# Moving three VectorE operations within a step of a gated attention block

## The chip, the cores and the metric

The kernel runs on one core of a Trainium2 chip. The metric is the device time of one execution in microseconds (us), the median of several runs.

## The reference

The input x is 2048 tokens x 512. It is normalised (layer norm) and goes through two branches, whose product is added to x.

```python
q, k, v = (_causal_dwconv(_silu(x @ W), conv_w) for each)   # 16 heads of 128, 4 taps
z, a, b = x @ Wz, x @ Wa, x @ Wb
q = q * cos + rot_half(q) * sin;  k = k * cos + rot_half(k) * sin
q = q / max(norm(q), 1e-12);      k = k / max(norm(k), 1e-12)
for s in range(4):                                          # lags 0 to 3
    attn = einsum('bshd,bshd->bsh', q, lag(k, s)) * scale
    gate = sigmoid(lag(a, s) * b)
    out = out + (attn * gate)[..., None] * lag(v, s)
out = out * rsqrt(mean(out * out) + eps) * norm_w * silu(z)
attn_branch = out @ Wout
ffn_branch  = (relu((x @ sign(up).T) * up_scale) @ sign(down).T) * down_scale * output_scale
x = x + attn_branch * silu(ffn_branch)
```

Each token looks at four keys only: its own and the three before it.

## The kernel before

The attention part, which takes the first two thirds of the time, works in steps. A step is one head h (16 of them) and one chunk g of 512 tokens (4 of them): 64 steps, numbered c = 4 h + g. The steps of the first two heads and of the last one are written out; those between are in a loop over the heads on every engine. Each engine has its own list of operations per step (the functions `step`), and semaphores tie the lists together. A chunk passes through several steps: in step c the projections are those of chunk c, while what comes behind them belongs to chunks c-1 to c-4.

- TensorE (`on_tensor`, L997, L1042, L1054, L1066), in step c: project q, k and v of chunk c (12 matmuls of 512 columns each, a product of split numbers in three parts), `turn_fold` (L1054: it turns the squares of chunk c-1), project z of chunk c-2, `sum_values` (L1042: values times coefficients of chunk c-3, both in float32), `score` (L1066: keys times queries of chunk c-2, blocks of 128 keys x 132 queries). `sum_values` waits for `coef_done`, the mask of the same chunk. `score` waits for `gated` of the chunk before, since both use one bank.
- ScalarE: SiLU of each projection out of PSUM (L662), a halo of three columns, the first tap as a scaled copy (L676), squares of q and k (L703, L704), SiLU of z (L711), a copy of the spill (L688).
- VectorE (`on_vector`): the remaining three taps of q, k and v (`conv_tap`, L812; called q1 to q3, k1 to k3, v1 to v3 here), the turn of v (L852), the products with cosine and sine (`rope`, L831 and L835), `sum_fold` (L842: reads the turned squares from PSUM and sums them to 4 norms for q and 4 for k per token row), `gate_scores` (L858: scores in PSUM times gates, into `coef`), `mask_band` (L867: `coef` times a band of ones), `join_out`, `make_o` and, in a head's last step, three splits of weights (L823), in its second step one.
- GpSimd (`on_gpsimd`): `roots` (L528 sets a floor under the norms, L532 raises to the power -1/2; it waits for `norms_done` of L842), `gate_keys` (L537), and in the next step the issues of accumulating DMAs (`fold_squares` L568, `add_swapped` L574 for rot_q and rot_k, `add_squares` L562), and between those of q and k `make_gates` (L548, L551, L556), which gives `gates_done`.
- SyncE's queue: `store_rq` (L402, L403, L405: the roots of chunk c-1 go to `rq_scratch` in DRAM), `load_rq` (L412: they come back shifted by rows for chunk c-2), which waits until the three stores have landed. Then the stores of o and the loads of v.

`make_gates` in step c handles chunk c-3 and needs the load of step c-1, which needs the roots of step c-1. `gate_scores` in step c needs those gates.

The order on each engine is written out by hand. Behind the attention come the FFN with the signs of the weights, and the output projection. They don't take part in the change.

Of the kernel before, what the change touches and what calls it, by code (L numbers as in the profile page):

```python
# [205 lines left out]
def attention(nc, env):  # L206
# [135 lines left out]
    def back(h, g, k):  # L342

        h2, g2 = (h, g - k) if g >= k else (h - 1, g - k + G)
        if isinstance(h2, int) and not 0 <= h2 < H:
            return None
        return h2, g2
# [11 lines left out]
    def is_start(h, g):  # L359
        return isinstance(h, int) and h == 0 and g == 0  # L360

    def is_end(h, g):
        return is_last(h) and g == G - 1

    def is_last(h):
        return isinstance(h, int) and h >= H - 1
# [404 lines left out]
    def on_vector(dve):  # L771
# [34 lines left out]
        def conv_tap(n, i, h, g, c):  # L806

            if i == 1:
                wait(dve, tap_done[n], c + 1)
            else:  # L810
                wait(dve, conv_done[n], DVE_TAPS[n] * c + i - 1)
            nc.vector.scalar_tensor_tensor(  # L812
                y[n][:, g % 2, :], u[n][:, g % 2, i:i + CH], cw[n][:, bass.ds(h * TAPS + i, 1)],
                y[n][:, g % 2, :], ALU.mult, ALU.add).then_inc(conv_done[n], 1)

        def join_out(g3, c):
            wait(dve, spill_saved, c - 2)
            nc.vector.tensor_tensor(out_begin, out_begin, carry[:, 2 * g3:2 * g3 + 2, :], ALU.add
                                    ).then_inc(out_joined, 1)

        def split_lo(n, h):
            wait(dve, whi_done[n], h + 1)
            nc.vector.tensor_tensor(w_lo[n][:, :, :], raw[n][:, :, :], w_hi[n][:, :, :].bitcast(fp32),  # L823
                                    ALU.subtract).then_inc(wlo_done[n], 1)

        def rope(n, i, g, c):

            wait(dve, conv_done[n], 3 * c + 3)
            if i == 0:
                wait(dve, scores_done, c - 3)  # L830
                op = nc.vector.tensor_tensor(rot[n][:, cols(g)], y[n][:, g % 2, :], cos[:, cols(g)], ALU.mult)  # L831
            else:
                if not (isinstance(c, int) and c < 2):
                    wait_rope(dve, n, g, c - 2)
                op = nc.vector.tensor_tensor(swapped[n][:, g % 2, :], y[n][:, g % 2, :], sin[:, cols(g)],  # L835
                                             ALU.mult)
            op.then_inc(rope_done[n], 1)

        def sum_fold(g1, c):
            wait(dve, turned_f, c)  # L840
            wait(dve, root_done, c - 2)
            nc.vector.tensor_reduce(norms[:, g1 % 2, :].rearrange("p (n b) -> p b n", b=BC),  # L842
                                    bank_tk[:, :].rearrange("p (b n d) -> p b n d", b=BC, n=2),
                                    AxisListType.X, ALU.add).then_inc(norms_done, 1)

        def turn_v(g1, k):

            wait(dve, conv_done["v"], 3 * (k + 1))
            if not (isinstance(k, int) and k < 2):
                wait_v(dve, g1, k - 2)  # L850
            v = y["v"][:, g1 % 2, :]
            nc.vector.transpose(v, v).then_inc(v_turned, 1)  # L852

        def gate_scores(g2, k):
            wait(dve, scores_done, k + 1)
            wait(dve, out_done, k - 1)
            wait(dve, gates_done, k + 1)
            nc.vector.tensor_tensor(  # L858
                coef[:, g2 % 2, :, :].rearrange("p b (a r) -> p b a r", r=LAGS),
                scores.rearrange("p b (a r) -> p b a r", r=LAGS),  # L860
                gates[:, :, None, :].broadcast_to([P, BC, BW // LAGS, LAGS]),
                ALU.mult).then_inc(gated, 1)

        def mask_band(g2, k):
            w = coef[:, g2 % 2, :, :]
            wait(dve, gated, k + 1)
            nc.vector.tensor_tensor(w, w, band[:, None, :].broadcast_to([P, BC, BW]), ALU.mult  # L867
                                    ).then_inc(coef_done, 1)

        def make_o(h3, g3, k):  # L870
            wait(dve, out_joined, k + 1)
            wait(dve, z_done, k + 1)

            wait(dve, o_stored[g3 % 2], 16 * (k // 2) if isinstance(k, int) else 8 * k - (8 if g3 % 2 else 0))
            nc.vector.scalar_tensor_tensor(
                o_buf[:, g3 % 2, :].rearrange("p (a n) -> p a n", a=2), out_sums,
                nw_sb[:, bass.ds(h3, 1)], z_act[:, g3 % 2, :].rearrange("p (a n) -> p a n", a=2),
                ALU.mult, ALU.mult).then_inc(o_done, 1)

        def step(h, g):  # L880
            c = h * G + g
            at1, at3 = back(h, g, 1), back(h, g, 3)
            conv_tap("q", 1, h, g, c)
            if at1:
                turn_v(at1[1], c - 1)
                rope("k", 0, at1[1], c - 1)
            conv_tap("q", 2, h, g, c)
            if at1:
                rope("k", 1, at1[1], c - 1)
            conv_tap("q", 3, h, g, c)  # L890
            conv_tap("k", 1, h, g, c)
            if at1:
                sum_fold(at1[1], c)
            conv_tap("k", 2, h, g, c)
            if at3:
                gate_scores(at3[1], c - 3)
                mask_band(at3[1], c - 3)
            conv_tap("k", 3, h, g, c)
            if is_start(h, g):
                dve.wait_ge(ab_turned, 1)  # L900
                nc.vector.tensor_copy(ab, bank_ab.rearrange("p (b n) -> p b n", b=NB)).then_inc(ab_done, 1)
                nc.vector.memset(bx[:, NB, :, :], 0.0).then_inc(bx_done, 1)
                dve.wait_ge(ab_done, 1)
                dve.wait_ge(const_in, 16)
                for r in range(LAGS):
                    nc.vector.tensor_scalar(bx[:, 0:NB, :, r], ab[:, :, H:AB], period[:, r:r + 1], None, ALU.mult
                                            ).then_inc(bx_done, 1)
            if is_start(h, g - 1):
                for i in range(2):
                    blocks = slice(i * HALF_NB, (i + 1) * HALF_NB)  # L910
                    dve.wait_ge(picked, i + 1)
                    nc.vector.tensor_tensor(
                        gate0[:, blocks, :].rearrange("p b (h r) -> p b h r", h=H),
                        pick_banks[i].rearrange("p (b h r) -> p b h r", b=HALF_NB, h=H),
                        ab[:, blocks, 0:H][:, :, :, None].broadcast_to([P, HALF_NB, H, LAGS]),
                        ALU.mult).then_inc(prod_done, 1)
            if g == 3 and not is_last(h):
                split_lo("q", h + 1)
            conv_tap("v", 1, h, g, c)
            if is_start(h, g):  # L920
                dve.wait_ge(tables_in, 32)
            rope("q", 0, g, c)
            conv_tap("v", 2, h, g, c)
            if at3:
                join_out(at3[1], c)
            conv_tap("v", 3, h, g, c)
            if g == 3 and not is_last(h):
                split_lo("k", h + 1)
            if at3:
                make_o(at3[0], at3[1], c - 3)  # L930
            rope("q", 1, g, c)
            if is_end(h, g):
                dve.wait_ge(squares_done, NC)
                nc.vector.tensor_tensor(fold[g % 2], fold[g % 2], other[g % 2], ALU.add).then_inc(folded_last, 1)
            if g == 3 and not is_last(h):
                split_lo("v", h + 1)
            if is_start(h, g - 1):
                for i in range(2):
                    part = gate0[:, i * HALF_NB:(i + 1) * HALF_NB, :]
                    dve.wait_ge(tanh_done, i + 1)  # L940

                    nc.vector.tensor_scalar(part, part, 1.0, 0.5 * SCALE, ALU.add, ALU.mult
                                            ).then_inc(gate_done, 1)
            if g == 1 and not (isinstance(h, int) and h == 0):
                split_lo("z", h)

        schedule(dve, step)
        turn_v(G - 1, NC - 1)
        rope("k", 0, G - 1, NC - 1)
# [656 lines left out]
```

## Time and profile before

| | |
|---|---|
| median of 3 runs | 1353.47 us (1352.22 to 1355.14) |
| the profiled execution | 1353.56 us |
| its span | 1351.7 us |
| TensorE busy | 1304.4 us, 96% |
| VectorE busy | 953.5 us, 71% |
| ScalarE busy | 720.7 us, 53% |
| GpSimd busy | 638.7 us, 47% |
| granted TensorE clock, mean | 0.996 of full speed |
| steps of the attention | 64, up to about 920 us |

The engines are named PE (TensorE), DVE (VectorE), ACT (ScalarE), POOL (GpSimd) and SP (SyncE); SPq is SyncE's queue. A line such as L858 is that of the kernel's file, where the operation is issued. The granted clock stands at its upper level in 39 or so of the page's 40 slices. In the attention part VectorE's busy share is about nine tenths, later two to four tenths.

### The profile page before, as it was taken

What the parts mean: (1) busy time and instruction counts of PE and PEld (TensorE: products, weight loads), DVE (VectorE), ACT (ScalarE), POOL (GpSimd) and SP (SyncE); (2) the same over time, 40 slices, a digit from 0 to 9 for tenths busy, and PEclk for the clock granted to TensorE, in tenths of its full rate; (3) what the DMA queues carried; (4) which work ended last, traced back from release to release, by engine and by line L of the source; (5) the groups of instructions that cost most, each with busy time, mean ns of one, the idle gap of its engine ahead of it and who ended that gap; (6) DMA issues with size and microseconds to landing.
All of it is one profiled execution on the core that took longest, in us unless ns stands there. A gap on an engine that the chain in (4) does not pass through costs nothing.

```text
span 1351.7 us, 22085 instructions
## 1 busy us (share of the span) xinstructions
PE 1304.4 (96%) x6312; PEld 1076.0 (80%) x6312; DVE 953.5 (71%) x1530; ACT 720.7 (53%) x1377; POOL 638.7 (47%) x827
## 2 busy tenths in 40 slices
PE   6989999999999999999999999998999999999998
PEld 5678888787878878888878888887888888888886
DVE  7888998989898998989898998985122223334342
ACT  5655665656666656566565666665543444422221
POOL 6367666767676666767666667765000000000001
PEclk9999999999999999999999999998999999999999
DMA  8368878878787877787787878677710101156544
GB/s 262 65 124 155 168 134 166 161 144 162 136 172 147 154 145 153 159 162 144 154 161 147 163 131 172 129 138 174 245 40 24 47 16 55 52 182 202 176 128 141
DMA packets 276876, 188.89 MB, mean 140 GB/s; under 512 B 167905, under 2 KB 204769, under 8 KB 276577
## 3 DMA queue, kind: packets, MB, share of 16 engines
q1 hardware_dynamic: 238064, 121.48, 32.8%
q0 software_dynamic: 38768, 66.87, 30.9%
q8 instruction: 23, 0.38, 0.1%
q14 instruction: 21, 0.16, 0.1%
HBM read 79.36 MB, written 42.08 MB: 90 GB/s over the span
## 4 chain that ended last, share of the span: by engine, by line
PE 51%; DVE 27%; issue 11%; ACT 6%; POOL 2%; DMA 2%; DVEq 1%; SPq 0%; POOLq 0%; ACTq 0%
PE bank L1491 13%; PE bank L997 11%; PE bank L1294 8%; PE bank L1281 8%; DVE y_q L812 6%; DVE y_k L812 6%; PE bank L1042 4%; PE bank L1066 3%; ACT y_q L676 3%; DVE rot_k L831 3%; DVE coef L858 3%; DVE coef L867 3%; ACT u_q L662 2%; DVE y_v L812 1%; DVEq L80 1%
## 5 line engine op out<-in xcount | busy, mean ns | idle before, releaser
L812 DVE SCALAR_TENSOR_TENSOR y_q<-u_q,cw_q,y_q 128x512 f32<-128x512 f32 x192 | 143.3, 746 | 86.4 <-ACT y_q L676 86.2
L1362 POOL TENSOR_TENSOR g_buf<-g_buf,up_raw 128x512 f32<-128x512 f32 x3 | 3.8, 1282 | 356.2 <-DVE g_buf L1422 356.2
L1270 DVE TENSOR_TENSOR hid_lo<-relu,hid_hi 128x512 fp32r<-128x512 f32 x64 | 44.3, 693 | 166.0 <-ACT hid_hi L1262 166.0
L574 POOL DMA_DIRECT2D rot_k<-swapped_k x128 | 107.4, 978 | 87.6 <-DVE swapped_k L835 79.2
L812 DVE SCALAR_TENSOR_TENSOR y_k<-u_k,cw_k,y_k 128x512 f32<-128x512 f32 x192 | 143.6, 748 | 1.3 <-ACT y_k L676 1.2
L812 DVE SCALAR_TENSOR_TENSOR y_v<-u_v,cw_v,y_v 128x512 f32<-128x512 f32 x192 | 143.3, 746 | 0.6
L574 POOL DMA_DIRECT2D rot_q<-swapped_q x128 | 107.5, 994 | 63.2 <-DVE swapped_q L835 59.8
L532 POOL TENSOR_TENSOR rnorm<-norms,neg_half 128x8 f32<-128x8 f32 x64 | 124.6, 1946 | 9.7 <-POOL norms L528 8.7
L1258 ACT ACTIVATE relu<-bank,us_sb 128x512 f32<-128x512 f32 x64 | 44.1, 690 | 127.0 <-PE bank L1281 119.8
L528 POOL TENSOR_SCALAR norms<-norms 128x8 f32<-128x8 f32 x64 | 103.9, 1624 | 4.4 <-DVE norms L842 4.4
L1382 ACT ACTIVATE hid_hi<-o_raw 128x512 fp32r<-128x512 f32 x64 | 40.2, 630 | 115.9 <-PE bank L1491 97.6
L1442 DVE TENSOR_TENSOR hid_lo<-o_raw,hid_hi 128x512 fp32r<-128x512 f32 x64 | 43.8, 690 | 79.9 <-ACT hid_hi L1382 79.9
L1042 PEld LDWEIGHTS bank<-coef,v_tok 128*128 128x128 f32 x512 | 63.2, 192 | 46.2 <-issue 40.6
L1491 PE MATMUL bank<-x_hi,hid_hi 128*128 128x512 f32 x256 | 99.6, 389 | 0.0
L1491 PE MATMUL bank<-x_hi,hid_lo 128*128 128x512 f32 x256 | 99.6, 389 | 0.0
L1491 PE MATMUL bank<-x_lo,hid_hi 128*128 128x512 f32 x256 | 99.6, 389 | 0.0
L662 ACT ACTIVATE u_q<-bank 128x512 f32<-128x512 f32 x64 | 38.4, 600 | 114.0 <-PE bank L997 114.0
L1042 PE MATMUL bank<-coef,v_tok 128*128 128x132 f32 x512 | 73.9, 288 | 21.6 <-DVE coef L867 20.5
L562 POOL DMA_DIRECT2D sq_sum<-out_sq x62 | 90.9, 1466 | 2.5 <-issue 2.5
L568 POOL DMA_DIRECT2D down_raw<-down_raw x63 | 59.3, 942 | 63.8 <-ACT down_raw L704 57.6
L662 ACT ACTIVATE u_v<-bank 128x512 f32<-128x512 f32 x64 | 38.4, 600 | 71.1 <-PE bank L997 71.1
L997 PE MATMUL bank<-x_hi,whi_z 128*128 128x512 f32 x256 | 75.5, 417 | 0.0
(189 smaller groups left out, 3546.4 us busy)
## 6 DMA issues: line engine op xcount, KB each, us to landing
rot_q<-swapped_q POOLq DMA_DIRECT2D x128, 128.0 KB, 4.1
v_scratch<-y_v SPq DMA_DIRECT2D x64, 256.0 KB, 3.1
rot_k<-swapped_k POOLq DMA_DIRECT2D x128, 128.0 KB, 3.4
v_tok<-v_scratch SPq DMA_DIRECT2D x256, 64.0 KB, 3.6
o_scratch<-o_buf SPq DMA_DIRECT2D x64, 256.0 KB, 3.0
o_raw<-o_scratch SPq DMA_DIRECT2D x64, 256.0 KB, 3.9
down_raw<-down_raw POOLq DMA_DIRECT2D x63, 256.0 KB, 3.4
sq_sum<-out_sq POOLq DMA_DIRECT2D x62, 256.0 KB, 4.4
```

The costliest lines, as they stand in the source:

```text
L528: nc.gpsimd.tensor_scalar(norms[:, g1 % 2, :], norms[:, g1 % 2, :], NORM_FLOOR, None, ALU.max).then_inc(floor_done, 1)
L532: nc.gpsimd.tensor_tensor(rnorm[:, g1 % 2, :], norms[:, g1 % 2, :], neg_half[:, 0:2 * BC], ALU.pow).then_inc(root_done, 1)
L562: nc.gpsimd.dma_start(sq_sum[:, cols(g)], squares, accum_op=ALU.add).then_inc(sq_added, 16)
L568: nc.gpsimd.dma_start(fold[g1 % 2], other[g1 % 2], accum_op=ALU.add).then_inc(folded, 16)
L574: nc.gpsimd.dma_start(rot[n][to:to + HALF, cols(g1)], swapped[n][frm:frm + HALF, g1 % 2, :], accum_op=ALU.add).then_inc(rope_added[n][g1 % ...
L662: nc.scalar.activation(u[n][:, g % 2, HALO:], bank[:, :], ACT.Silu).then_inc(silu_done[n], 1)
L812: nc.vector.scalar_tensor_tensor(y[n][:, g % 2, :], u[n][:, g % 2, i:i + CH], cw[n][:, bass.ds(h * TAPS + i, 1)], y[n][:, g % 2, :], ALU.m ...
L997: last = nc.tensor.matmul(bank[:, :], w[n][:, i % KT, :], part[:, i % KT, cols(g)], start=(i == 0), stop=(i == TERMS - 1))
L1042: last = nc.tensor.matmul(two[:, b // 2, at:at + BW], v_tok[:, g3 * BC + b, :], coef[:, g3 % 2, b, :], start=(b % 2 == 0), stop=(b % 2 == ...
L1281: last = nc.tensor.matmul(up_bank(n, j), up_group(j // WG)[:, t, j % WG * P:(j % WG + 1) * P], part[:, t, bass.ds(n * CH, CH)], start=(k = ...
L1294: last = nc.tensor.matmul(acc_of(n)[b], part[:, j % HS, b * P:(b + 1) * P], down_group(j // WG)[:, j % WG, :], start=(j == 0 and part is h ...
L1491: last = nc.tensor.matmul(sums[b], part[:, h % HS, b * P:(b + 1) * P], wo_tile(w, h // KT, h % KT), start=(h == 0 and k == 0), stop=(h == ...
```

## The change

In VectorE's step, `gate_scores` moves from behind k2 to between q3 and k1. `mask_band`, which stood right behind it, moves to between k1 and k2. `sum_fold` moves from between k1 and k2 to between k2 and k3. Everything else stays, the order behind the last step too.

```diff
             conv_tap("q", 3, h, g, c)
+            if at3:
+                gate_scores(at3[1], c - 3)
             conv_tap("k", 1, h, g, c)
+            if at3:
+                mask_band(at3[1], c - 3)
+            conv_tap("k", 2, h, g, c)
             if at1:
                 sum_fold(at1[1], c)
-            conv_tap("k", 2, h, g, c)
-            if at3:
-                gate_scores(at3[1], c - 3)
-                mask_band(at3[1], c - 3)
             conv_tap("k", 3, h, g, c)
```

## Rows read from the trace of the kernel before

**Rows 1.** The page: engine totals, and shares of the chain that ended last.

```profile
PE 1304.4 (96%) x6312; PEld 1076.0 (80%) x6312; DVE 953.5 (71%) x1530; ACT 720.7 (53%) x1377; POOL 638.7 (47%) x827
PE 51%; DVE 27%; issue 11%; ACT 6%; POOL 2%; DMA 2%; DVEq 1%; SPq 0%; POOLq 0%; ACTq 0%
```

**Rows 2.** Waits, 200 to 840 us: engine, line, releaser, total, times, longest.

```profile
PE bank L1042 <- DVE coef L867: 17.4, 46, 0.7
DVE y_q L812 <- ACT y_q L676: 63.6, 47, 2.0
```

**Rows 3.** Timeline of TensorE, one step in the loop: start, us, engine, line, what.

```profile
501.84 1.14 PE L1042 MATMUL bank<-coef,v_tok 128*128 128x132 f32 x8 [0.28 <-DVE coef L867]
...
510.98 1.07 PE L997 MATMUL bank<-x_lo,whi_v 128*128 128x512 f32 x4
511.89 0.60 PE L1054 MATMUL bank<-const,down_raw 128*128 128x128 f32 x4
...
514.17 1.07 PE L997 MATMUL bank<-x_lo,whi_z 128*128 128x512 f32 x4
515.51 1.14 PE L1042 MATMUL bank<-coef,v_tok 128*128 128x132 f32 x8 [0.28 <-DVE coef L867]
```

**Rows 4.** TensorE's timeline, a head's first step, and a step written out.

```profile
541.60 1.07 PE L997 MATMUL bank<-x_lo,whi_z 128*128 128x512 f32 x4
543.27 0.91 PE L1042 MATMUL bank<-coef,v_tok 128*128 128x132 f32 x6 [0.61 <-DVE coef L867]
...
900.01 1.07 PE L997 MATMUL bank<-x_lo,whi_z 128*128 128x512 f32 x4
901.20 1.17 PE L1042 MATMUL bank<-coef,v_tok 128*128 128x132 f32 x8
```

**Rows 5.** Timeline of VectorE around the moved operations, and the next q1.

```profile
511.89 0.75 DVE L812 SCALAR_TENSOR_TENSOR y_k<-u_k,cw_k,y_k 128x512 f32<-128x512 f32 x1
512.55 0.68 DVE L842 TENSOR_REDUCE norms<-bank 128x8 f32<-128x512 f32 x1
513.15 0.74 DVE L812 SCALAR_TENSOR_TENSOR y_k<-u_k,cw_k,y_k 128x512 f32<-128x512 f32 x1
513.81 0.70 DVE L858 TENSOR_TENSOR coef<-bank,gates 128x528 f32<-128x528 f32 x1
514.55 0.71 DVE L867 TENSOR_TENSOR coef<-coef,const 128x528 f32<-128x528 f32 x1
515.17 0.75 DVE L812 SCALAR_TENSOR_TENSOR y_k<-u_k,cw_k,y_k 128x512 f32<-128x512 f32 x1
...
521.82 0.75 DVE L812 SCALAR_TENSOR_TENSOR y_q<-u_q,cw_q,y_q 128x512 f32<-128x512 f32 x1 [1.92 <-ACT y_q L676]
```

**Rows 6.** Timeline of GpSimd and SyncE's queue from the norms to the gates.

```profile
513.59 1.76 POOL L528 TENSOR_SCALAR norms<-norms 128x8 f32<-128x8 f32 x1
515.51 1.94 POOL L532 TENSOR_TENSOR rnorm<-norms,neg_half 128x8 f32<-128x8 f32 x1 [0.16 <-POOL norms L528]
517.48 0.32 SPq L402 DMA_DIRECT2D rq_scratch<-rnorm  x1
519.39 0.57 SPq L412 DMA_DIRECT2D rq_win<-rq_scratch  x1
520.48 1.65 POOL L574 DMA_DIRECT2D rot_q<-swapped_q  x2 [0.71 <-DVE swapped_q L835]
522.58 0.24 POOL L548 TENSOR_TENSOR rq_win<-rq_win,const 128x32 f32<-128x32 f32 x1 [0.45 <-DMA rq_win<-rq_scratch]
523.20 0.66 POOL L556 TENSOR_TENSOR gates<-rq_own,gate_k 128x16 f32<-128x16 f32 x1
```

**Rows 7.** The same chain in the last head, where its parts lie differently.

```profile
902.55 0.62 POOL L528 TENSOR_SCALAR norms<-norms 128x8 f32<-128x8 f32 x1
...
906.56 1.96 POOL L574 DMA_DIRECT2D rot_q<-swapped_q  x2
907.20 0.57 SPq L412 DMA_DIRECT2D rq_win<-rq_scratch  x1
912.52 0.24 POOL L548 TENSOR_TENSOR rq_win<-rq_win,const 128x32 f32<-128x32 f32 x1 [4.00 <-DMA rq_win<-rq_scratch]
```

## The prediction

> **What bounds the kernel now.** I read the page first. TensorE is busy 96% of the span, yet only about half of the chain that ended last is TensorE; a quarter is VectorE [rows 1]. So TensorE is nearly full, and in every step something else releases it once. The table of waits in the attention part says where: TensorE waits 46 times in 640 us, always at L1042 (the weighted sum of the values), for VectorE's L867 (the mask) [rows 2]. VectorE in turn waits at q's first tap for ScalarE. This is a ring, once in a step: L1042, scores, projection of q (TensorE); SiLU and first tap (ScalarE); then in VectorE's order q1, turn of v, k's two rope products, q2, q3, k1, L842 (sum of the folded squares), k2, L858 (gates), L867 (mask); then L1042 again. "q1" to "v3" are conv taps.
>
> **What TensorE loses per step.** The records of matmuls overlap, so I compare starts. Four 512-column matmuls that are followed at once take 510.98 to 511.89 = 0.91 us (v's last group, then the turn of the squares). In front of L1042 the same four take 514.17 to 515.51 = 1.34 us: 0.43 us lost [rows 3]. Of the 60 steps c = 3 to 62, 39 are of this kind (0.43 to 0.54, mean 0.45). In the first step of a head it is 541.60 to 543.27, so 1.67 - 0.91 = 0.76 us (13 steps), because VectorE also had the three splits of weights to do. In the steps written out before and behind the loop it is 900.01 to 901.20, so 0.28 us (8 steps, 0.20 to 0.37) [rows 4]. The sum is 39 x 0.45 + 13 x 0.76 + 8 x 0.28 = 17.6 + 9.9 + 2.2 = 29.7 us. The period from L1042 to L1042 is 515.51 - 501.84 = 13.67 us; without the loss TensorE alone makes 13.24 us. The mean period is 13.24 + 29.7/60 = 13.74 us.
>
> **The change part by part.** No instruction is added or removed; three are moved on VectorE. None issues a DMA, and nothing is moved on the queues of SyncE or GpSimd.
>
> 1. *Gates two places and mask about two places earlier.* Now the order from k1 is k1 511.89, L842 512.55, k2 513.15, L858 513.81, L867 514.55, end 515.26 [rows 5]. Steps between starts are 0.66, 0.60, 0.66, 0.74 us. After: L858, k1, L867, k2, L842, k3 from the same point, so L867 starts 0.62 (a start to the next independent one, estimated from L867 to k3's place and the 0.60 above) + 0.66 = 1.28 us behind L858 and ends 0.71 later: 1.99 us behind the point against 3.37 us. The mask is done 1.38 us earlier. The ring had only 0.43 us (0.76) to give back, so TensorE becomes the bound, and the mask is ready about 0.9 us before L1042 wants it: q1 starts 6.31 us behind the last L1042 (521.82 - 515.51) [rows 3, 5], the point is 3.79 us behind q1, so the mask ends at 6.31 + 3.79 + 1.99 = 12.1 us of 13.24. In the first step of a head VectorE starts some 0.2 us later: 12.3 us, and still early. Between a mask's end and L1042's start 0.25 us go by (515.26 to 515.51); that still fits. Worth: up to -29.7 us. The lower bound of what this gives: if going from the projections' matmuls to L1042 costs TensorE 0.1 us a step even without a wait (v's end shows no such start-up; 0.1 us is my estimate from L1042's own record, 1.14 against the 1.07 of most groups in rows 3), 6 us of it stay. I take the full value, since v's last group to the turn of the squares is the nearest row.
>
> 2. *L842 later: L858, L867 and k2 now stand ahead of it.* Its end moves from 1.34 us behind the point to 0.62 + 0.66 + 0.62 + 0.66 + 0.68 = 3.24 us: +1.9 us for GpSimd's L528 (floor) and L532 (power), then SyncE's stores and load of the norms (L402, L412), then the gates (L548 to L556), which L858 of the next step needs. Before, L842 stood ahead of L858 and the two made no ring. Now they do: L842 -> roots -> store -> load -> gates -> L858 -> k1, L867, k2, L842. Its length decides. Rows of now: L528 0.36 us behind L842's end, store 3.89 behind that, load 1.91 behind the store, L548 3.19 behind the load, gates done 1.28 us later (523.86) [rows 5, 6]: 10.6 us. With 0.12 to L858 and 3.24 back to L842's end that would be 14.0 us, longer than 13.24, and longer than today's 13.67. But three pieces shrink. L528 now starts late, behind two other issues of GpSimd; behind an L842 that comes later it can follow in about 0.2 us. L528 takes 1.76 us now, to 0.09 us behind the end of the mask at 515.26; where no mask runs beside it, it takes 0.62 [rows 7] and behind k3 and v1 I expect 0.6 us. L532 stays at 1.94. So the store comes 0.2 + 0.6 + 0.15 + 1.94 = 2.9 us behind L842's end and not 4.25. The ring is then 2.9 + 1.91 + 3.0 + 1.3 + 0.12 + 3.24 = 12.5 us, under 13.24 by 0.7 us. Worth: 0 in the long run.
>
>    This rests on what holds GpSimd up beside the mask. The Trainium skill ("SBUF — State Buffer", section on two separate sides) says that VectorE and GpSimd share a port pair as an exclusive lock, and that a VectorE operation with two SBUF inputs blocks a GpSimd operation that reads SBUF, until some 115 ns behind its end. The 0.09 us above agree. If instead L528 really needed its 1.76 us, the ring would be 13.7 us and the gain of the change about nothing.
>
> 3. *The store and load meet other transfers.* The load (L412) now starts 1.09 us ahead of rot_q's accumulating transfers (519.39, 520.48) [rows 6]. Both hang on VectorE's order: the rot_q issue stays 5.27 us behind the new end of L842, the load goes to 2.9 + 1.9 = 4.8. So the lead falls to about 0.4 us, and in steps whose stores land 0.4 us later, to about nothing. That matters: at 906.56 rot_q was issued 0.64 us ahead of the load, and L548 ran 5.32 us behind the load instead of 3.2 [rows 7]. With a lead above zero I see no delay.
>
> 4. *The last head.* Behind its second step the load comes late already. There L858, now wanted 1.9 us earlier, will wait for the gates, and k1, L867, k2, L842 stand behind it on VectorE, L1042 behind them. From the 5.32 us of rows 7: gates some 2 us later than wanted less the 0.9 us of room, once, and again partly in the drain: +1 to +2 us, I take +1.2.
>
> Sum: -29.7 + 1.2 = -28.5 us. The profiled execution took 1353.56 us with a span of 1351.7, 0.1 us above the median of 1353.47; so 1353.5 - 28.5 = **1325.0 us**.
>
> **Rivals.**
> *A. The ring through the gates becomes the bound (slower).* If the load falls behind rot_q in every step, L548 runs 5.3 us behind the load: 2.9 + 1.91 + 5.3 + 1.3 + 0.12 + 3.24 = 14.8 us. That is 1.0 us over the mean period of 13.74, times 60 = +62 us: about 1415 us. It decides from a ring of 13.74 us, that is from 1.2 us more than my 12.5. For it: the lead is only 0.4 us by my sum. Against: it would need to be negative, and even at half a microsecond behind not every load need be slow.
> *B. The load is late in one phase of four* (the step after a head's first, whose stores land later). There gates come 2 us late, of which 0.9 are covered: about +1.1 us in 15 steps, +16 us: 1341 us.
> *C. TensorE's wait at L1042 is mostly its own way of passing four waits*, 0.26 us between the mask's end and its start whatever comes when. Then only 0.17 of 0.43 us go (0.5 in a head's first step): 39 x 0.19 + 13 x 0.5 + 8 x 0.05 = 14 us, 1340 us. Against: the other waits of the step, as before the turn of the squares, cost no gap.
> *D. The change does nothing*, because another release of TensorE, hidden behind this one, is as late. The views show no other wait of TensorE; the next is v's SiLU with more than 1 us of room.
>
> **How the numbers follow.** Forecast (1320 to 1332): 0.66. B or C (1332 to 1346): 0.17. D: 0.04. A, also in part, ending over 1356: 0.13. The range must hold 0.8; it goes from 1319 (the drain gains a little too) to 1345, and leaves A and D out. The measurement can tell about 0.2%, 2.7 us, from no change. Faster 0.83, same 0.04, slower 0.13.
>
> **What would show it.** Right: TensorE's waits at L1042 for L867 all but gone in the loop; L1042 to L1042 13.2 to 13.3 us, also in a head's first step; L528 at 0.6 us; L842 ending near L1042's start; L858 without idle time before it; VectorE's wait at q1 1 to 1.5 us still there. Wrong by A or B: L858 idle for GpSimd's gates and GpSimd's L548 idle for the load by 2 us and more. Wrong by C: starts 0.2 us late with the mask long done. What would upset it most is a lead of the load over rot_q that comes out negative.

## The result, and the profile after

The changed kernel takes 1388.1 us (median of 4, 1384.9 to 1391.1) beside 1353.7 us for the kernel before on the same chip: ratio 1.0254, 95% interval 1.0221 to 1.0286. That is 34 us slower; 1325 us was forecast, with 1319 to 1345 as the range. The profiled execution took 1390.7 us with a span of 1388.9.

The page's totals and its chain that ended last, of the changed kernel (compare [rows 1]). The functions stand one or more lines lower in the file from here on where an edit added lines (L1043 is the old L1042).

```profile
PE 1310.2 (94%) x6312; PEld 1083.2 (78%) x6312; DVE 951.5 (69%) x1530; ACT 720.6 (52%) x1377; POOL 641.7 (46%) x827
PE 34%; DMA 23%; POOL 18%; DVE 12%; issue 7%; SPq 3%; ACT 1%; POOLq 1%; DVEq 0%; ACTq 0%
```

Busy times are nearly the same, but the chain is another. TensorE's share fell from 51% to 34%; transfers (2% before), GpSimd (2%) and SyncE's queue now make up 44% of it. This is the ring through the gates, which the prediction had as its slower rival. The waits between 200 and 840 us in the changed kernel show who stands still (compare [rows 2]; total in us, times, longest):

```profile
POOL rq_win L548 <- DMA rq_win<-rq_scratch: 117.0, 42, 4.3
...
DVE coef L858 <- POOL gates L556: 74.5, 41, 3.0
...
PE bank L1043 <- DVE coef L867: 36.0, 29, 2.0
```

GpSimd waits for the load of the norms 42 times, 2.8 us each; VectorE waits for the gates at L858, where before it never did; and TensorE's wait for the mask, which the change was to take away, has doubled. One turn of the ring, from the chain of waits of the changed kernel (start, length, what; pieces under 0.2 us are left out):

```profile
525.11 0.55 POOL norms L528
525.82 2.54 POOL rnorm L532
528.38 0.33 SPq L402
528.75 0.34 SPq L403
529.13 1.32 DMA rq_scratch<-rot_q
530.47 5.00 DMA rq_win<-rq_scratch
535.54 0.24 POOL rq_win L548
535.87 0.21 POOL rq_own L551
536.15 0.24 POOL gates L556
536.51 0.71 DVE coef L858
...
539.16 0.61 DVE norms L842
539.98 0.55 POOL norms L528
```

From L528 to L528 it is 539.98 - 525.11 = 14.87 us. A third of it is one transfer of 16 KB, which takes 5.0 us to land. What goes on beside it stands in the timeline of GpSimd and SyncE's queue in the same turn:

```profile
530.11 1.71 POOL L574 DMA_DIRECT2D rot_q<-swapped_q  x2
...
535.54 0.24 POOL L548 TENSOR_TENSOR rq_win<-rq_win,const 128x32 f32<-128x32 f32 x1 [3.72 <-DMA rq_win<-rq_scratch]
```
```profile
530.47 0.58 SPq L412 DMA_DIRECT2D rq_win<-rq_scratch  x1
```

rot_q was issued at 530.11, ahead of the load at 530.47. Before, the load was ahead, 519.39 against 520.48 [rows 6].

The following table is worked out from the timelines between 200 and 840 us: medians over the steps whose place in the head is the same. "Lead" is the start of rot_q's issue less the start of the load, negative where the load comes second; "landing" is from the load's start to L548's. The step kinds are numbered by c mod 4, so that kind 0 is a head's first step. "Wait at L858" is whether the next step's L858 stands idle for these gates, and the last column is from this step's L1042 to the next one.

| kernel | step kind | L532 | L842's end to store | store to load | lead | landing | wait at L858 | to the next L1042 |
|---|---|---|---|---|---|---|---|---|
| before | 1 | 1.94 | 4.24 | 1.91 | 1.09 | 3.08 | no | 13.70 |
| before | 2 | 1.94 | 4.24 | 1.91 | 1.09 | 3.16 | no | 13.72 |
| changed | 0 | 2.53 | 3.48 | 3.37 | -1.39 | 3.08 | yes | 13.69 |
| changed | 1 | 2.53 | 3.48 | 1.91 | -0.17 | 5.19 | yes | 14.82 |
| changed | 2 | 2.54 | 3.48 | 1.91 | -0.17 | 5.58 | yes | 15.19 |
| changed | 3 | 2.53 | 4.08 | 1.90 | +0.43 | 2.99 | yes | 14.48 |

The mean step between 200 and 840 us went from 13.80 to 14.48 us; over all the steps from c = 3 to 62 it went from 13.77 to 14.37 us, and 59 times these 0.60 us are 35 us, the whole of the loss. In kinds 1 and 2 the load is 0.2 us behind rot_q and lands 2 us late. In kind 0 the stores land late as well (3.37 us), so the load isn't even issued until 1.4 us behind rot_q. In kind 3 the load leads and lands in 3 us.

The granted TensorE clock has a small part in this. Between 200 and 840 us it stood at the lower of its two levels (1.2 and not 2.4 GHz) four times in the changed kernel, for 3.4 us each, and never in the kernel before. This is one of the four stretches; the granted clock, as a share of full speed, is the 0.50 near its end:

```profile
554.50:557.90 3.40, 3.40 (x17) 3.40 (x16) 3.40 (x7) 1.77 (x4) 2.52 (x3) 0.50 0.69 114
```

Each of the four lies in a step of kind 3, behind a step of 15.2 to 15.4 us in which TensorE had waited. These four steps took 14.9 us against the 14.5 us of their kind: 2 us of the 34 at most.

### The profile page after: what moved, and what is told of

The parts are those of the page before. It is cut to its first block, busy times and chain, and to the rows that moved or that the text cites. A ratio compares the mean times of both kernels' runs of the same rounds, so it can differ in the third digit from the quotient of the medians.

```text
span 1388.9 us, 22098 instructions
## 1 busy us (share of the span) xinstructions
PE 1310.2 (94%) x6312; PEld 1083.2 (78%) x6312; DVE 951.5 (69%) x1530; ACT 720.6 (52%) x1377; POOL 641.7 (46%) x827
## 4 chain that ended last, share of the span: by engine, by line
PE 34%; DMA 23%; POOL 18%; DVE 12%; issue 7%; SPq 3%; ACT 1%; POOLq 1%; DVEq 0%; ACTq 0%
DMA rq_win<-rq_scratch 16%; PE bank L1492 12%; POOL rnorm L532 11%; PE bank L1295 8%; PE bank L1282 8%; DVE y_k L812 6%; DMA rq_scratch<-rnorm 5%; POOL norms L528 3%; DVE coef L858 3%; PE bank L998 2%; DVE norms L842 2%; DMA rq_scratch<-rot_q 1%; SPq L403 1%; POOL rq_win L548 1%; SPq L402 1%
## 5 line engine op out<-in xcount | busy, mean ns | idle before, releaser
L532 POOL TENSOR_TENSOR rnorm<-norms,neg_half 128x8 f32<-128x8 f32 x64 | 160.6, 2510 | 9.6 <-POOL norms L528 8.6
L858 DVE TENSOR_TENSOR coef<-bank,gates 128x528 f32<-128x528 f32 x64 | 45.2, 707 | 102.8 <-POOL gates L556 102.8
L1043 PE MATMUL bank<-coef,v_tok 128*128 128x132 f32 x512 | 74.2, 290 | 41.9 <-DVE coef L867 41.6
L1043 PEld LDWEIGHTS bank<-coef,v_tok 128*128 128x128 f32 x512 | 66.0, 196 | 60.1 <-issue 55.4
L548 POOL TENSOR_TENSOR rq_win<-rq_win,const 128x32 f32<-128x32 f32 x64 | 21.9, 342 | 162.7 <-DMA rq_win<-rq_scratch 162.7
L998 PE MATMUL bank<-x_hi,whi_q 128*128 128x512 f32 x252 | 75.6, 423 | 3.1 <-DVE wlo_q L823 2.5
L1067 PE MATMUL bank<-rot_q,rot_k 128*128 128x132 f32 x512 | 72.0, 285 | 5.4 <-DVE coef L858 5.4
```

Source lines behind the costliest of these rows:

```text
L532: nc.gpsimd.tensor_tensor(rnorm[:, g1 % 2, :], norms[:, g1 % 2, :], neg_half[:, 0:2 * BC], ALU.pow).then_inc(root_done, 1)
L858: nc.vector.tensor_tensor(coef[:, g2 % 2, :, :].rearrange("p b (a r) -> p b a r", r=LAGS), scores.rearrange("p b (a r) -> p b a r", r=LAGS ...
L998: last = nc.tensor.matmul(bank[:, :], w[n][:, i % KT, :], part[:, i % KT, cols(g)], start=(i == 0), stop=(i == TERMS - 1))
L1043: last = nc.tensor.matmul(two[:, b // 2, at:at + BW], v_tok[:, g3 * BC + b, :], coef[:, g3 % 2, b, :], start=(b % 2 == 0), stop=(b % 2 == ...
L1067: last = nc.tensor.matmul(scores[:, b, :], rot["k"][:, at:at + P], rot["q"][:, at:at + BW], start=True, stop=True)
```

## The experiments

My theory after the result: the load L412 is issued just behind rot_q's transfers and lands behind them, because L532 takes 0.6 us longer than I took it to; that makes the ring the bound. Rivals: the ring is too long whatever rot_q does; the loss is contention outside the ring; a late `sum_fold` costs by itself.

| kernel | edit against the changed kernel, if no other is named | us | ratio to before, 95% interval |
|---|---|---|---|
| changed | | 1388.1 | 1.0254 (1.0221 to 1.0286) |
| 1 | rot_q issued behind the gates | 1402.3 | 1.0362 (1.0337 to 1.0387) |
| 2 | order k1, sum_fold, gates, mask, k2 | 1328.0 | 0.9803 (0.9786 to 0.9820) |
| 3 | q's cosine product behind v2 | 1326.7 | 0.9787 (0.9768 to 0.9805) |
| 4 | without the load | 1320.4 | 0.9744 (0.9725 to 0.9763) |
| 5 | order gates, k1, mask, sum_fold, k2 | 1324.8 | 0.9795 (0.9778 to 0.9811) |
| 6 | against the kernel before: only sum_fold moved | 1360.1 | 1.0059 (1.0038 to 1.0080) |
| 7 | work added ahead of rot_q's issue | 1339.5 | 0.9897 (0.9880 to 0.9913) |
| 8 | against kernel 3: work added ahead of the store | 1427.8 | 1.0552 (1.0534 to 1.0570) |
| 9 | rot_q's transfers a quarter as large | 1336.4 | 0.9872 (0.9856 to 0.9887) |
| 10 | against kernel 5: split of k's weights earlier | 1317.5 | 0.9728 (0.9715 to 0.9742) |

**1. rot_q behind the gates.**

```diff
             if at := back(h, g, 1):
                 fold_squares(at[1], c)
-                add_swapped("q", at[1], c - 1)
             if at := back(h, g, 3):
                 make_gates(at[1], c - 3)
             if at := back(h, g, 1):
+                add_swapped("q", at[1], c - 1)
                 add_swapped("k", at[1], c - 1)
```

> The changed kernel, with one more move: GpSimd issues the two accumulating transfers of rot_q behind the gates (L556), not ahead of them. Theory 1 (the ring through the gates is long only because the load L412 is issued 0.17 us behind rot_q and lands behind it, 5.2 to 5.8 us later): the load lands 3 us or less behind its issue, the ring is 0.21 + 3.27 + 1.91 + 3.0 + 0.83 + 0.13 + 3.39 = 12.7 us, under TensorE's 13.24, and the time is 1325 to 1335. Rival (the ring is long by GpSimd's roots and the stores, whatever rot_q does): within 5 us of 1388. Third: rot_q itself comes too late for the scores, TensorE waits at L1066 for the transfer: 1350 or more.

It took 1402.3 us: the third outcome. The load landed fast (2.1 to 3.0 us behind its issue in the median of each kind of step), as theory 1 says. But rot_q itself came too late, which the waits of this kernel show:

```profile
PEld bank L1067 <- DMA rot_q<-swapped_q: 46.4, 22, 3.6
PE bank L1067 <- DMA rot_q<-swapped_q: 42.1, 22, 3.4
```

So this run alone decides nothing on the time, but it bars the plain remedy: rot_q can't be pushed far back.

**2. No ring: sum_fold ahead of the gates, k2 behind the mask.**

```diff
+            conv_tap("k", 1, h, g, c)
+            if at1:
+                sum_fold(at1[1], c)
             if at3:
                 gate_scores(at3[1], c - 3)
-            conv_tap("k", 1, h, g, c)
             if at3:
                 mask_band(at3[1], c - 3)
             conv_tap("k", 2, h, g, c)
-            if at1:
-                sum_fold(at1[1], c)
```

> VectorE's order k1, sum_fold, gate_scores, mask_band, k2, k3: k2 alone goes behind the mask. sum_fold stands ahead of the gates as before the change, so there is no ring through the gates on VectorE. Theory 1 (ring): no wait at L858 for the gates, load and rot_q 1.1 us apart as before; the mask is done 0.66 us earlier than before, more than the 0.43 us of an ordinary step: 1325 to 1332. If TensorE's 0.25 us between the mask's end and L1042 is its own way of passing four waits, only about half comes: 1340.

1328.0 us, in the range of theory 1. TensorE has no wait at L1042 left between 200 and 840 us, and the period is 13.16 us in three kinds of step out of four. The 0.25 us between the mask's end and L1042 were not TensorE's own: they are gone as well (rival C of the prediction falls).

**3. q's cosine product behind v2.**

```diff
             conv_tap("v", 1, h, g, c)
-            rope("q", 0, g, c)
             conv_tap("v", 2, h, g, c)
+            rope("q", 0, g, c)
```

> The changed kernel, with VectorE's product of q with the cosine (L831) behind v2 and not ahead of it, so that it does not run beside the start of GpSimd's power (L532, 2.53 us now, 1.94 us before). Theory 1: L532 falls to 1.7 to 2.0 us, the load then starts some 0.4 us ahead of rot_q and not 0.17 us behind, and L548 runs 3 us behind the load: half a microsecond of GpSimd gives back most of the loss, 1325 to 1345. Rival (the length of the ring is a plain sum, no order of transfers in it): 0.6 us in each of 60 steps, 1388 - 36 = 1352.

1326.7 us: 61 us faster than the changed kernel, by the swap of two neighbours on VectorE. L532 fell from 2.53 to 1.93 us, as the lines of the tile of the reciprocal norms say, first of the changed kernel, then of this one (shortest/median/longest in ns):

```profile
L532 POOL TENSOR_TENSOR rnorm<-norms,neg_half x44: 2527/2532/2538, 204.9 to 828.1; 128x8 f32<-128x8 f32 x44
```
```profile
L532 POOL TENSOR_TENSOR rnorm<-norms,neg_half x48: 1923/1929/1934, 209.7 to 836.0; 128x8 f32<-128x8 f32 x48
```

With it the lead went from -0.17 to +0.50 us in kinds 1 and 2, and the landing from 5.2 and 5.6 to 2.6 and 2.7 us. A plain sum of 0.6 us in each step would have given 1352 us; the other 25 us come with the faster landings. The tile of the loaded window, in the changed kernel and in this one (GpSimd's waits for it in us, times; then the landings):

```profile
  DMA rq_win<-rq_scratch: 117.0, 42
DMA to landing us min/median/max: 2.1/3.8/5.7
```
```profile
  DMA rq_win<-rq_scratch: 34.2, 46
DMA to landing us min/median/max: 2.1/2.6/3.6
```

**4. Without the load.**

```diff
-            sp.dma_start(rq_win[:, g2 % 2, :, :]..., runs).then_inc(arrived, 16)
+            sp.sem_inc(arrived, 16)
```

> The changed kernel without the load L412: the window of the norms is set once at the start to a constant, and the semaphore is raised by SyncE's queue where the load stood, still behind the landing of the stores. Left out: the reciprocal norms of q in the gates. All else is as in the changed kernel. Theory 1: the ring is 0.21 + 3.27 + 1.9 + 0.3 + 0.83 + 0.13 + 3.39 = 10.0 us, TensorE is the bound with 13.24 us a step, and the time is my forecast's 1320 to 1330. Rival (what slows the changed kernel is contention of transfers or of VectorE and GpSimd outside this ring): over 1350.

1320.4 us, with everything else of the change in place. (The window is set to a constant once at the start; the lines for that are left out above.) The load is what the ring hangs on, and no contention outside of it costs anything near 60 us. With the change as it stands, no faster load can give more than this.

**5. Mask, then sum_fold, then k2.**

```diff
             if at3:
                 mask_band(at3[1], c - 3)
-            conv_tap("k", 2, h, g, c)
             if at1:
                 sum_fold(at1[1], c)
+            conv_tap("k", 2, h, g, c)
             conv_tap("k", 3, h, g, c)
```

> VectorE's order gate_scores, k1, mask_band, sum_fold, k2, k3: as in the changed kernel, but sum_fold one tap earlier. The ring through the gates stands, shorter by k2's 0.6 us; the store and the load come 0.6 us earlier while rot_q stays. Theory 1: lead of the load about +0.5 to +1 us, ring 12.1 us or less, TensorE the bound: 1320 to 1330. Rival (any ring through the gates costs, or gates this early find them late): 1350 or more.

1324.8 us. The ring still exists here, yet it is shorter than TensorE's step; the lead is +1.09 us in kinds 1 and 2. Gates and mask can go where the change puts them; it is sum_fold one tap later that tips it, 63 us for 0.6 us.

**6. sum_fold alone.** The edit is against the kernel before.

```diff
             conv_tap("k", 1, h, g, c)
+            conv_tap("k", 2, h, g, c)
             if at1:
                 sum_fold(at1[1], c)
-            conv_tap("k", 2, h, g, c)
             if at3:
                 gate_scores(at3[1], c - 3)
                 mask_band(at3[1], c - 3)
```

> One part of the change alone: sum_fold behind k2, gate_scores and mask_band behind it as before (order k1, k2, sum_fold, gate_scores, mask_band, k3). No ring, since sum_fold stands ahead of the gates; the mask ends where it ended before, so TensorE loses its 0.43 and 0.76 us a step as before. Theory 1: 1350 to 1357, no waits for gates at L858. Rival (a later sum_fold is what costs, by itself): 1365 or more.

1360.1 us: 3 us over the range of theory 1, and below the rival's 1365. No wait for the gates; a later sum_fold does not cost 34 us by itself. The 7 us have another place. TensorE's wait for the mask grew:

```profile
PE bank L1043 <- DVE coef L867: 24.6, 46, 0.9
```

That is 24.6 us against 17.4 [rows 2], 0.16 us a step. k1 and k2, which now follow each other, work on the same tile, and k2 starts 0.78 us behind k1 in this kernel; behind an operation on another tile the next starts after 0.60 or 0.66 us, and behind the one that made its input after 0.74 us [rows 5]. The mean period grew by 0.16 us, from 13.80 to 13.96 us, in 60 steps 9.6 us. That two such neighbours are the cause was not tried by itself.

**7. Work added ahead of rot_q's issue.** `spend(3)` is three times `nc.gpsimd.tensor_tensor(idle[:, i, :], window[:, :], window[:, :], ALU.mult)`, a product of 128x8 that nobody reads.

```diff
                 fold_squares(at[1], c)
+                wait(pool, rope_done["q"], 2 * c)
+                spend(3)
                 add_swapped("q", at[1], c - 1)
```

> The changed kernel with work added: ahead of the issue of rot_q's transfers GpSimd waits for VectorE's product as it does anyway, then makes three products of 128x8 that nobody reads (0.2 to 0.3 us each by L551's 0.22). The store and the load stay where they are in the changed kernel. Theory 1 (order of load and rot_q): the load now leads by 0.4 to 0.7 us and not -0.17, it lands within 3 us, the ring is 12.7 us and the time falls to 1325 to 1345, although GpSimd has more to do. Rival (length of GpSimd's part of the ring, or contention in general): 1385 to 1400.

1339.5 us: 49 us faster than the changed kernel, with three useless instructions more in every step. L532 (2.53 us) and the way to the store (3.48 us) are unchanged; in kinds 1 and 2 the lead went from -0.17 to +0.18 and +0.09 us, less than I had expected, and the landing to 2.6 us. The ring is still just the bound (wait at L858: 20.7 us in 47 steps, period 13.39 us), which is why it isn't 1325: L532 stays long, and from the start of L548 to the end of the gates it takes 1.9 us here in the median, against 0.84 us in the changed kernel. This speaks most plainly against the rival that GpSimd's share of the ring is simply too long.

The medians hide that the order of the two issues does not decide by itself. In the changed kernel 17 of the 19 loads issued 0.1 to 0.4 us behind rot_q took 5.0 to 5.7 us to land, one 4.0 and one 2.6. Yet in kernel 3 seven loads issued 0.17 to 0.48 us behind landed in 2.5 to 3.0 us, and in this kernel seven issued 0.14 to 0.53 us behind in 2.1 to 3.3 us. What tells the fast ones of these from the slow ones is not shown. Of the loads issued ahead of rot_q, in all the kernels that have the whole of it, none took longer than 3.3 us.

**8. Work added ahead of the store, in kernel 3.**

```diff
             nc.gpsimd.tensor_scalar(norms[:, g1 % 2, :], ..., NORM_FLOOR, None, ALU.max)
+            if not is_last(h1):
+                spend(3)
             wait(pool, floor_done, c)
```

> The kernel with q's cosine product behind v2, which took 1326.7 us, with the same three small products of GpSimd put between the floor (L528) and the power (L532) in all heads but the last, so that the stores and the load come 0.6 to 0.9 us later and rot_q does not. Theory 1: the load's lead over rot_q goes from +0.5 to about -0.2 us, the load lands 5 us or more behind its issue again, and the time goes back to 1370 to 1395. Rival (plain sum): the ring there is 9.1 to 9.4 + 3.4 = 12.6 us, with 0.7 more 13.3, at TensorE's 13.24: no more than 1336.

1427.8 us: 101 us more than kernel 3 and beyond the range of theory 1, which had the direction but not the size. The way from L842's end to the store is 4.27 us in kinds 1 and 2, 1.4 us longer than in kernel 3 and twice what I had meant (the three products take 1.4 us here, and 0.8 us in kernel 7); the lead is -0.4 us, the landing 5.2 us. In kind 3 the load is 0.14 us behind as well and lands in 2.9 us. In kinds 1 and 2 the sum holds: the ring grew by 1.4 us by the products and by 2.6 us by the landing, less the room it had.

**9. A quarter of rot_q.**

```diff
+                part = CH // 4 if n == "q" else CH
-                nc.gpsimd.dma_start(rot[n][to:to + HALF, cols(g1)], swapped[n][frm:frm + HALF, g1 % 2, :], ...)
+                nc.gpsimd.dma_start(rot[n][to:to + HALF, g1 * CH:g1 * CH + part],
+                                    swapped[n][frm:frm + HALF, g1 % 2, 0:part], ...)
```

> The changed kernel with rot_q's two transfers cut to a quarter of their columns (128 of 512), issued where they are. Left out: three quarters of q's rotation. Theory 1, first form (the load lands late because the data of rot_q's transfers, 4 us of them, stand ahead of it on the DMA engines): L548 runs 3 us or so behind the load, not 5.2 to 5.8, the ring falls under TensorE's step, and the time is 1320 to 1340. Second form (it is the issue on GpSimd's queue and not the data): the load lands as late as in the changed kernel, over 1375.

1336.4 us, in the first form's range. Lead (-0.17 us), L532 (2.53 us) and the way to the store are those of the changed kernel; only the bytes ahead of the load are fewer. The landing falls to 3.5 to 3.7 us, and the longest of all from 5.7 to 3.8:

```profile
DMA to landing us min/median/max: 2.1/3.3/3.8
```

So the load waits behind rot_q's data, not behind its issue. In the changed kernel the 17 slow loads fit this: each landed within 0.3 us ahead of rot_q's second transfer. Some 0.9 to 1.1 us over the 2.6 us of kernel 3 are left, with a quarter of the data.

**10. A version faster than both.** This is kernel 5, with the split of k's weights one tap earlier in a head's last step. Once L1042 no longer waits, TensorE's only wait in kernel 5 was this, 13 times:

```profile
PE bank L998 <- DVE wlo_k L823: 3.8, 13, 0.3
```

```diff
-            conv_tap("v", 3, h, g, c)
             if g == 3 and not is_last(h):
                 split_lo("k", h + 1)
+            conv_tap("v", 3, h, g, c)
```

> The order gate_scores, k1, mask_band, sum_fold, k2, k3, which took 1324.8 us, with one more move: in a head's last step the split of k's weights stands ahead of v3, not behind it. In that step TensorE's period was 13.72 us against 13.15 in the others, with a wait of 0.29 us for this split (L823) at k's projection. The split is ready 0.66 us earlier: the 0.57 us go in 14 steps: 1324.8 - 8 = 1317. If TensorE's wait moves to v's split or to q's SiLU instead, 1321 to 1325.

1317.5 us (median of 5), 36 us under the kernel before. The period is 13.15 or 13.16 us in all four kinds of step. What is left of TensorE's waits between 200 and 840 us is one line:

```profile
PE bank L998 <- DVE wlo_q L823: 0.2, 1, 0.2
```

## Why the prediction was wrong

**What TensorE loses: right.** The ring TensorE, ScalarE, VectorE, back to L1042 was the bound, and its price was 29.7 us. Without the wait TensorE's step is 13.15 us (kernels 2, 3, 5; I had 13.24), and kernels 5 and 10 give back 28 and 36 us. Into a head's first step only 0.3 us of the 0.76 us came (from 14.04 to 13.73 us in kernel 5), since k's split is next there. I had named no such wait; kernel 10 shows it.

**Part 1, gates and mask earlier: right.** In kernel 5 they stand where the change puts them, and it takes 1324.8 us.

**Part 2, the ring through the gates: the step that failed first is "L532 stays at 1.94".** It is 2.53 us in each of the 44 steps between 200 and 840 us. L528 did shrink as said (0.54 us, for 0.6; 1.14 us in kind 3). The way from L842's end to the store is 3.48 us, not 2.9. With that alone the ring would be 13.1 us, still under TensorE's step; it became the bound by what part 3 had wrong as well. I had priced what stops running beside GpSimd's two operations when they move, the mask, but not what they move next to: v1 and q's cosine product. In the changed kernel that product starts 0.32 us behind L532 (526.14 against 525.82), in the kernel before 1.0 us behind it. This timeline is VectorE's in the changed kernel:

```profile
525.47 0.75 DVE L812 SCALAR_TENSOR_TENSOR y_v<-u_v,cw_v,y_v 128x512 f32<-128x512 f32 x1
526.14 0.69 DVE L831 TENSOR_TENSOR rot_q<-y_q,cos 128x512 f32<-128x512 f32 x1
526.74 0.75 DVE L812 SCALAR_TENSOR_TENSOR y_v<-u_v,cw_v,y_v 128x512 f32<-128x512 f32 x1
```

Kernel 3 moves nothing but this product and L532 is 1.93 us. So the product at this place is what makes it long, but its start is not the whole condition: twice in the kernel before it started 0.33 us behind L532 too, and L532 took 1.94 us:

```profile
350.62 1.94 POOL L532 TENSOR_TENSOR rnorm<-norms,neg_half 128x8 f32<-128x8 f32 x1 [0.16 <-POOL norms L528]
350.95 0.69 DVE L831 TENSOR_TENSOR rot_q<-y_q,cos 128x512 f32<-128x512 f32 x1
```

The rule of the Trainium skill that the prediction quoted ("SBUF — State Buffer", section "SBUF: two separate sides") names the risk, since the product has two inputs in SBUF, and I did not apply it at the new place. It would not have given the price. By the Trainium skill the one of the two that starts first holds the shared pair for its whole length and the other is blocked. Here L532 starts first, the product takes the 0.69 us that it always takes, and it is L532 that grows, by 0.6 us; and v1 and v2, which have two inputs in SBUF as well, leave L532 at 1.93 us in kernel 3. The same holds for L528 and the mask, on which the prediction read this rule: L528 had started first (513.59 against 514.55 [rows 5, 6]), and in kernel 6 it takes 0.55 us though the mask starts 0.43 us behind it.

**Part 3, the lead: the mechanism was named, the size was wrong by the same 0.6 us.** "The lead falls to about 0.4 us": it was -0.17 us in kinds 1 and 2. "At 4.8" for the load was 5.4 us behind L842's end; rot_q came 5.2 us behind it, as forecast (5.27). The price of a negative lead, from [rows 7], was 5.3 us of landing; measured 5.2 and 5.6. So rival A happened, not in every step but in two kinds of four, with a third slow by its stores: rival A's 1415 us for every step, 1388 measured. I gave A 0.13. That was too little for a margin of 0.4 us which rested on an L532 and an L528 that nobody had measured at their new places, with some 60 us behind it: kernels 3 and 7 lie on its one side, the changed kernel and kernel 8 on the other. The prediction's own caution, that not every load issued behind need be slow, came true.

**Part 4, the last head**, can't be told apart here: in the changed kernel the ring was the bound all along. Kernel 4, without the load, is 4 us faster than kernel 5, which bounds what the load costs there and elsewhere in the best case.

**Rival B** had its delay in one kind of step; it was in three. **Rival C** falls by kernel 2.

## What to carry to other kernels

When an operation moves past a wait, write down the ring that it closes and price each link at its new place: what runs beside it there counts as much as what ran beside it before. Where two transfers are issued within half a microsecond of each other and the small one is awaited, a shift of a few tenths can cost more than the shift itself (here 63 us of the time for 0.6 us a step); a margin thinner than the uncertainty of the sum deserves far more than an eighth of the probability. Let the small, awaited transfer be issued first, if need be by delaying the large one a little, but not by so much that its own reader waits.

## What the runs showed of the hardware

- A load of 16 KB that was issued ahead of 256 KB of accumulating transfers on GpSimd's queue took 2.0 to 3.3 us to land: 367 loads, between 200 and 840 us, in all the kernels with the whole of rot_q. The 36 loads that took more than 4.5 us (17 in the changed kernel, 19 in kernel 8) were all issued behind them, by 0.13 to 0.81 us, though the two are issued on different queues. Not every load behind them is slow (kernels 3, 7 and 8). With 64 KB ahead of it the load took 3.5 to 3.7 us (kernel 9).
- GpSimd's power on 128x8 takes 1.93 to 1.94 us in kernel 3 and in the kernel before, and 2.53 us when VectorE's product of two SBUF tiles starts 0.30 to 0.32 us behind it (the changed kernel, 44 of 44); with the product 0.33 us behind it was 1.94 us (the kernel before, twice). With nothing of VectorE beside it, at the end of the attention of the kernel before, it took 1.67 us. The floor on 128x8 takes 0.54 us beside taps (the changed kernel); beside gates and mask it takes 1.76 us in the kernel before and 0.55 us in kernel 6, where they lie otherwise in time.
- Three small products of GpSimd in each step made a kernel 49 us faster in one place (kernel 7 against the changed kernel) and 101 us slower in another (kernel 8 against kernel 3).
- TensorE's granted clock stood at the lower level for 3.4 us at a time, between 200 and 840 us, nine times in kernel 8, six times in kernel 1 and four times in the changed kernel, the three slowest; in the kernel before and in all the others it did not.
